# First block, seam and fusion steps of a filter-and-transformer kernel: loads and waits reordered

## Time and profile before

| | us |
|---|---|
| median of 3 runs | 1001.25 (999.52 to 1002.82) |
| the profiled execution | 999.17 |
| its span | 997.3 |
| TensorE busy | 905.2 (91%) |
| VectorE busy | 834.9 (84%) |
| ScalarE busy | 699.3 (70%) |
| GpSimd busy | 122.3 (12%) |
| mean granted clock of TensorE | 0.976 |

### The profile page before, as it was taken

One profiled execution on the slowest core, in us unless ns is written; L12 is line 12 of the kernel. 1 busy time (PEld: TensorE's weight loads), 2 busy tenths in 40 slices (PEclk: granted clock), 3 DMA queues, 4 the chain that ended last, 5 costly groups with the idle time before them and its releaser, 6 DMA issues.

```text
span 997.3 us, 18874 instructions
## 1 busy us (share of the span) xinstructions
PE 905.2 (91%) x6960; PEld 700.2 (70%) x6960; DVE 834.9 (84%) x1160; ACT 699.3 (70%) x2252; POOL 122.3 (12%) x147
## 2 busy tenths in 40 slices
PE   5489999999999999999999997889998999999997
PEld 4267777777777777777777775767675766667675
DVE  2999999999999999999999998987899599352443
ACT  2666876976877877877876875757767686767842
POOL 6201011011011011101101111101010111000000
PEclk9699999999999999999999999999998999999999
DMA  7311120031010121010220010000001000100000
GB/s 173 113 35 28 66 89 19 22 122 45 18 45 17 32 90 39 17 46 14 70 80 11 17 38 11 12 22 12 27 17 38 17 22 17 44 27 2 17 1 32
DMA packets 24925, 39.00 MB, mean 39 GB/s; under 512 B 4001, under 2 KB 20609, under 8 KB 23553
## 3 DMA queue, kind: packets, MB, share of 16 engines
...
q0 software_dynamic: 384, 1.05, 0.5%
...
HBM read 22.21 MB, written 5.24 MB: 28 GB/s over the span
## 4 chain that ended last, share of the span: by engine, by line
DVE 47%; PE 25%; ACT 16%; issue 9%; DMA 2%; POOL 1%; SPq 0%; DVEq 0%; POOLq 0%; ACTq 0%
ACT prob L1086 7%; PE ps_t L849 7%; DVE f L1726 4%; DVE f L1753 4%; PE ps_m L860 4%; DVE f L1748 4%; DVE p L1738 4%; DVE f L1757 4%; DVE neg_max L1762 4%; DVE f L1743 3%; ACT u L1073 3%; DVE f L1721 2%; DVE f L1710 2%; PE ps_s L796 2%; DVE f L1699 2%
## 5 line engine op out<-in xcount | busy, mean ns | idle before, releaser
L1086 ACT ACTIVATE prob<-ps_s,neg_max 128x128 f32<-128x128 f32 x512 | 181.3, 408 | 7.3 <-DVE neg_max L1762 7.3
L1086 ACT ACTIVATION_READ_ACCUMULATOR prob<-ps_s,neg_max 128x1 f32 x512 | 126.6, 249 | 0.0
L655 PE MATMUL ps_t<-w,hidT 128*128 128x256 f32 x512 | 125.7, 383 | 0.0
L1094 ACT ACTIVATE probT<-ps_t 128x512 f32<-128x512 f32 x128 | 81.1, 634 | 44.3 <-PE ps_t L601 28.7
L655 PEld LDWEIGHTS ps_t<-w,hidT 128*128 128x128 f32 x512 | 91.1, 190 | 12.1 <-ACT hidT L1168 3.0
L849 PE MATMUL ps_t<-km,w_fc 128*128 128x384 f32 x256 | 93.9, 503 | 1.0 <-ACT km L1282 1.0
L601 PE MATMUL ps_t<-ident,prob 128*128 128x128 f32 x512 | 81.5, 283 | 12.9 <-ACT prob L1086 6.7
L601 PEld LDWEIGHTS ps_t<-ident,prob 128*128 128x128 f32 x512 | 60.0, 144 | 36.6 <-issue 14.7
L1762 DVE TENSOR_REDUCE neg_max<-ps_s 128x8 f32<-128x1024 f32 x64 | 77.5, 1211 | 4.6 <-PE ps_s L591 4.6
L1341 ACT ACTIVATE prob<-ps_s,neg_max 128x128 f32<-128x128 f32 x192 | 53.8, 376 | 22.6 <-DVE neg_max L1935 22.2
L849 PEld LDWEIGHTS ps_t<-km,w_fc 128*128 128x128 f32 x256 | 47.5, 195 | 26.8 <-issue 3.7
...
## 6 DMA issues: line engine op xcount, KB each, us to landing
...
w_attn<-in_w_attn SPq DMA_DIRECT2D x4, 768.0 KB, 5.4
...
```

The costliest lines, as they stand in the source:

```text
L655: last = mm(ps_t[:, 0, D * t:D * t + D], hidT[:, m, P * t:P * t + P], w2[:, m], start=False, stop=(m == MC - 1), skip_group_check=True)
L1086: last = A(prob[:, n % 2, hh], ps_s[n % 2][:, hh], ACT.Exp, scale=-1.0, bias=neg_max[:, n % 2, hh:hh + 1], accum_out=den)
L1094: A(probT[:, 4 * half:4 * half + 4].rearrange("p h k -> p (h k)"), ps_t[:, 1], ACT.Copy).then_inc(s["act_pT"], 1)
```

## The change

What it does, part by part:

- SP: taps and positions are issued from ScalarE's queue. The filter's column weights (`vf[:, 1]`) come before its row weights, each with a semaphore of its own, and both ahead of the projections, which now stand behind the first row shift. The rest of layer 0's weights moves behind `rows_above(0)`, `w2` behind `rows_above(1)`; the images of the next pair go from a block's first iteration to its second.
- GpSimd: the last six gathers wait for the projections to have landed. The masks are one head wide (`[P, 2, P]`), and their readers repeat them by a broadcast.
- TensorE, SP and ScalarE's first tanh wait for eight constants (`N_EARLY`), not nine; ScalarE's first tanh did not wait for constants before.
- VectorE: `first_step` begins with the head masks and the first filter operations, ahead of the positions; `head_max(0, 0)` to `(0, 2)` move behind other filter operations; in block 0 the two `normalise` stand among the divergence operations; in block 15 they stand ahead of `divergence_out`.
- TensorE: four `hold_clock` ahead of `fuse_queries(0)`, three behind `tile_scores(0, 0)`.
- ScalarE: `values_in(n + 1)` ahead of `norm_y(n)` in `fuse_step`.

```diff
@@ -86,7 +86,7 @@
         ident = sb("ident", [P, P])
         ident_h = sb("ident_h", [P, P], BF16)
         ones = sb("ones", [P, 4 * P])
-        mask = sb("mask", [P, 2, 4, P], BF16)
+        mask = sb("mask", [P, 2, P], BF16)
         head_mask = sb("head_mask", [P, 2])
         pow_half = sb("pow_half", [P, 4])
         row_mask = sb("row_mask", [P, 4])
@@ -251,37 +251,28 @@
-        N_CONST = 8 + 1
+        N_EARLY = 8
+        N_CONST = N_EARLY + 1
...
         @block.sync
         def _(sp):
             sp.dma_start(tokens[:], d["tokens"]).then_inc(s["l_tok"], 16)
-            sp.dma_start(taps[:, 0:18], d["nabla_w"].partition_broadcast(P)).then_inc(s["l_taps"], 16)
-            sp.dma_start(taps[:, 18:36], d["div_w"].partition_broadcast(P)).then_inc(s["l_taps"], 16)
-            sp.dma_start(pe[:], d["pe"]).then_inc(s["l_pe"], 16)
             load_images = lambda k: sp.dma_start(o_all[:, k], d["o"][2 * k:2 * k + 2].rearrange("b (p r) c -> (b p) r c", r=RPP))
             load_images(0).then_inc(s["l_img"], 16)
-            sp.dma_start(w_attn[:, :, 0:3 * D], d["w_attn"][0][:, :, 0:3 * D]).then_inc(s["l_qkv"], 16)
-            for img in range(2):
-                for comp in range(2):
-                    sp.dma_start(vf[64 * img:64 * img + 64, comp], d["vf"][comp].rearrange("(p r) c -> p r c", r=RPP)).then_inc(s["l_vf"], 16)
+            for comp, loaded in ((1, "l_vf"), (0, "l_vf_rows")):
+                for img in range(2):
+                    sp.dma_start(vf[64 * img:64 * img + 64, comp], d["vf"][comp].rearrange("(p r) c -> p r c", r=RPP)).then_inc(s[loaded], 16)
             def rows_below(it):
                 if it < ITERS * PAIRS:
                     sp.wait_ge(s["act_tanh"], it + 1)
                     for at in (0, 64):
                         sp.dma_start(u[at:at + 63, RPP, 0:IMG], u[at + 1:at + 64, 0, 0:IMG]).then_inc(s["halo_u"], 16)
-            sp.wait_ge(s["c_pool"], N_CONST)
+            sp.wait_ge(s["c_pool"], N_EARLY)
             rows_below(0)
-            sp.wait_ge(s["g_emb"], 16 * (B - 2))
-            sp.dma_start(w_attn[:, :, 3 * D:4 * D], d["w_attn"][0][:, :, 3 * D:4 * D]).then_inc(s["l_wc"], 16)
-            sp.dma_start(cols[:], d["cols"]).then_inc(s["l_vec"], 16)
-            sp.dma_start(rows_last[:], d["rows_last"].partition_broadcast(P)).then_inc(s["l_vec"], 16)
-            sp.dma_start(b1[:], d["b1"][0]).then_inc(s["l_bc"], 16)
-            sp.dma_start(w1[:], d["w1"][0]).then_inc(s["l_w1"], 16)
-            sp.dma_start(w2[:], d["w2"][0]).then_inc(s["l_w2"], 16)
+            sp.dma_start(w_attn[:, :, 0:3 * D], d["w_attn"][0][:, :, 0:3 * D]).then_inc(s["l_qkv"], 16)
             sp.wait_ge(s["c_general"], 1)
             which = sp.value_load(general[0:1, 0:1], min_val=0, max_val=1)
...
@@ -348,11 +339,24 @@
+            def first_weights():
+                sp.wait_ge(s["g_emb"], 16 * (B - 2))
+                sp.dma_start(w_attn[:, :, 3 * D:4 * D], d["w_attn"][0][:, :, 3 * D:4 * D]).then_inc(s["l_wc"], 16)
+                sp.dma_start(cols[:], d["cols"]).then_inc(s["l_vec"], 16)
+                sp.dma_start(rows_last[:], d["rows_last"].partition_broadcast(P)).then_inc(s["l_vec"], 16)
+                sp.dma_start(b1[:], d["b1"][0]).then_inc(s["l_bc"], 16)
+                sp.dma_start(w1[:], d["w1"][0]).then_inc(s["l_w1"], 16)
+
+            def first_ff_out():
+                sp.dma_start(w2[:], d["w2"][0]).then_inc(s["l_w2"], 16)
+
             for k in range(BLOCKS):
                 it, its, l = sum(BLOCK_ITERS[:k]), BLOCK_ITERS[k], k // PAIRS
                 for i in range(its):
                     rows_above(it + i)
-                    if i == 0 and k < PAIRS - 1:
+                    if k == 0:
+                        (first_weights if i == 0 else first_ff_out)()
+                    if i == 1 and k < PAIRS - 1:
                         load_images(k + 1).then_inc(s["l_img_rest"], 16)
                     if i == 0 and k % PAIRS == PAIRS - 1 and l + 1 < LAYERS:
                         load_projections(l + 1)
@@ -422,6 +427,7 @@
                 if b == 1:
                     const(pool.memset(v[:], 0.0))
                     assert c == N_CONST
+                    pool.wait_ge(s["l_qkv"], 16)
             pool.wait_ge(s["g_emb_first"], 32)
@@ -432,10 +438,10 @@
             for first in range(2):
                 for half in range(2):
                     m = mask[64 * half:64 * half + 64, first]
-                    const(pool.affine_select(out=m, in_=m, compare_op=ALU.is_gt, fill=MASKED, base=0, pattern=[[0, 4], [1, P]], channel_multiplier=-1))
-                    const(pool.affine_select(out=m, in_=m, compare_op=ALU.is_ge, fill=MASKED, base=WIN, pattern=[[0, 4], [-1, P]], channel_multiplier=1))
+                    const(pool.affine_select(out=m, in_=m, compare_op=ALU.is_gt, fill=MASKED, base=0, pattern=[[1, P]], channel_multiplier=-1))
+                    const(pool.affine_select(out=m, in_=m, compare_op=ALU.is_ge, fill=MASKED, base=WIN, pattern=[[-1, P]], channel_multiplier=1))
                     if first and half == 0:
-                        const(pool.affine_select(out=m, in_=m, compare_op=ALU.is_ge, fill=MASKED, base=-WIN, pattern=[[0, 4], [1, P]], channel_multiplier=0))
+                        const(pool.affine_select(out=m, in_=m, compare_op=ALU.is_ge, fill=MASKED, base=-WIN, pattern=[[1, P]], channel_multiplier=0))
             const(pool.memset(v_f[:, :, :, HD:], 1.0))
             for t in (vT_f[:, 0:WIN], kT_f[:, 0:WIN]):
                 const(pool.memset(t, 0.0))
@@ -709,6 +715,8 @@
                 if a + 1 < BLOCKS:
                     queries(a + 1)
                 else:
+                    for _ in range(4):
+                        hold_clock(BLOCKS)
                     fuse_queries(0)
                     fuse_values(0)
@@ -783,9 +791,9 @@
                 else:
                     pe_.wait_ge(s["f_q"], n + 1)
                     pe_.wait_ge(s["f_k"], n + 1)
-                    m = mask[:, 1].rearrange("p a k -> p (a k)")
+                    m = mask[:, 1].unsqueeze(1).to_broadcast([P, 4, P])
                     for hb in range(2):
-                        mm(quad[hb], ident_h[:], m, start=True, stop=False, skip_group_check=True)
+                        mm(quad[hb].rearrange("p (a k) -> p a k", a=4), ident_h[:], m, start=True, stop=False, skip_group_check=True)
                 for c in range(FKV):
                     for r in range(2):
                         to = P * (2 * c + r)
@@ -869,6 +877,8 @@
                 carry_attn(LAST)
                 project_out(LAST)
                 tile_scores(0, 0)
+                for _ in range(3):
+                    hold_clock(BLOCKS)
                 tile_turn(0, 0, 0)
                 tile_turn(0, 0, 1)
                 turn_ffn(LAST)
@@ -1044,7 +1054,7 @@
                 ff_out(f, 1, range(0, 4))
                 ff_out(f, 2, range(0, 4))
-            pe_.wait_ge(s["c_pool"], N_CONST)
+            pe_.wait_ge(s["c_pool"], N_EARLY)
             for i in range(40):
                 tr(ps_t[:, 1, P * (i % 4):P * (i % 4) + P], ident[:], ident[:])
             first_step()
@@ -1063,6 +1073,10 @@
         def _(act):
             A = act.activation
+            act.dma_start(taps[:, 0:18], d["nabla_w"].partition_broadcast(P)).then_inc(s["l_taps"], 16)
+            act.dma_start(taps[:, 18:36], d["div_w"].partition_broadcast(P)).then_inc(s["l_taps"], 16)
+            act.dma_start(pe[:], d["pe"]).then_inc(s["l_pe"], 16)
+
             def first_tanh(pair):
                 A(u[:, 0:RPP, 0:IMG], o_all[:, pair], ACT.Tanh).then_inc(s["act_tanh"], 1)
@@ -1137,6 +1151,8 @@
                 scaled_rows(k, ps_t[:, 0], rstd, shift).then_inc(s["h_ready"], 1)
             def keys_out(k, g):
+                if k == 0:
+                    act.wait_ge(s["c_heads"], 1)
                 act.wait_ge(s[f"pe_k{g}"], k + 1)
                 for o in range(2):
                     last = A(km[:, g, :, o], quad[2 + g][:, 0:D].rearrange("p (t k) -> p t k", t=2), ACT.Copy, scale=head_mask[:, o:o + 1])
@@ -1252,6 +1268,7 @@
                 filter_out(1)
                 queries_out(1)
+            act.wait_ge(s["c_pool"], N_EARLY)
             act.wait_ge(s["l_img"], 16)
             first_tanh(0)
             act.wait_ge(s["c_general"], 1)
@@ -1344,7 +1361,7 @@
             def tile_mask(n, t):
                 act.wait_ge(s["f_exp"], 2 * TT * n + 2 * t)
                 for hb in range(2):
-                    last = A(quad[hb], mask[:, 0].rearrange("p a k -> p (a k)"), ACT.Copy)
+                    last = A(quad[hb].rearrange("p (a k) -> p a k", a=4), mask[:, 0].unsqueeze(1).to_broadcast([P, 4, P]), ACT.Copy)
                 last.then_inc(s["f_mask"], 1)
             def tile_sink(n, t):
@@ -1456,8 +1473,8 @@
                 x_out(n + 1)
                 z_last(n - 1)
                 keys_biased(n + 1)
+                values_in(n + 1)
                 norm_y(n)
```

(54 more changed lines are left out.)

9 lines of the change are left out of this document (5 added, 4 removed).

## The result

The changed kernel takes **997.07 us** (median; 993.73 to 1002.02), the kernel before beside it 1001.67 (998.75 to 1006.41), in 20 runs each: ratio 0.9949 [0.9935, 0.9962], some 5.1 us faster. Forecast was 992.3, so the sign is right and about four tenths of the gain is missing. The median lies 0.07 above the upper end of the forecast's range (997); the ratio, put on the 1001.25 that the forecast started from, gives 996.1, inside it. The profiled execution took 997.71 with a span of 996.0, 1.3 less than that of the kernel before.

What follows compares the result with a forecast made beforehand. VectorE was taken to lead the chain (47%, TensorE 25%). Gains of 6.9 (head), 0.8 (seam) and 1.2 (fusion steps) sum to 8.9 us, taking the median from 1001.25 to 992.3, range 987.5 to 997.

Steps and rivals of the forecast that it cites:

- The bound: Whole kernel: VectorE leads the chain; what the first block ends earlier, the end of the text stage is earlier.
- the term of 6.9 for the head: Kernel start: earlier loads and new order start block 1's first operation at 52.7 instead of 59.57, 6.9 us earlier.
- the forecast's signs of being wrong: Start, block 0: block 1 starting after 56, keys after 16, or gathers spaced over 2 us.
- so the tanh runs from 5.0 to 6.1: Kernel start: SP issues the image 1.41 us earlier, so ScalarE's first tanh runs from 5.0 to 6.1.
- keys at 13.6: Kernel start: the keys' products begin at 13.6 us, just behind the projections' landing, taken as 13.2.
- Rival 2: Cold TensorE at the start: clock falls before the keys, products up to twice as long; 2.4 lost, 994.7; chance 0.14.
- The 3 us wait ahead of normalise(0, 0): Block 0, at 44 to 47 us: in the new order VectorE waits some 3 us instead of working.
- The seam, 0.8: About 611 to 629 us: fillers and earlier normalise end queries 2.8 earlier; VectorE next in line, so 0.8 kept.
- The swap, 1.2: Fusion steps 2 and 4: value copy ahead of the norm falls into ScalarE's wait, 0.6 each, 1.2 us.
- Rival 1: Kernel start: projections land late, at 18.3, held by row shifts and filter weights; 4.1 lost, 997.2; chance 0.08.
- Rival 3: Block 0: six gathers each wait out a VectorE operation of 1.2, last lands 7 us later; 995.3; chance 0.12.
- Rival 4: Block 0: gathers get nowhere until VectorE pauses at 26; 14.6 lost against 8.9 won, 1006.9; chance 0.03.

Runs made afterwards that it cites:

- experiment 4: Changed kernel with taps and positions issued by SP behind the four filter weights instead of by ScalarE: 1001.41 us, ratio 0.9991 to the kernel before.
- experiment 10: Changed kernel with taps and positions issued by SP ahead of the image, as in the kernel before: 999.79 us, ratio 0.9975 to the kernel before.
- experiment 12: Kernel of experiment 8 with 16 instead of 24 later fillers and the small loads by SP ahead of the image: 991.15 us, ratio 0.9892.
- experiment 8: Changed kernel, table loaded early, block 0's normalises behind divergence_out(1), fillers 64 for 40 plus 24 behind the text rows' turn: 995.18 us, ratio 0.9914.
- experiment 11: Kernel of experiment 8 with small loads ahead of the image and projections issued ahead of the wait for the tanh: 993.18 us, ratio 0.9914.
- experiment 6: Kernel before with only the seam's edit: seven hold_clock fillers, block 15's normalises ahead of divergence_out: 999.82 us, ratio 0.9988.
- experiment 7: Kernel before with only values_in ahead of norm_y in the fusion steps: 1001.88 us, ratio 0.9992.
- experiment 3: Changed kernel with block 0's two normalises put back behind divergence_out(1): 995.88 us, ratio 0.9933 to the kernel before.
- experiment 5: Changed kernel with seam fillers, block 15's normalises and values_in as before, leaving the new start and masks: 1000.58 us, ratio 0.9986.
- experiment 9: Changed kernel without GpSimd's wait for the projections ahead of the last six gathers: 999.89 us, ratio 0.9979 to the kernel before.
- experiment 1: The changed kernel run again, nothing altered: 998.48 us, ratio 0.9962 to the kernel before.
- experiment 2: Changed kernel with a tiny activation ahead of ScalarE's waits, to load the activation table early: 998.55 us, ratio 0.9969 to the kernel before.

## Why the prediction was partly right

**The bound: right.** Block 1's start does carry through. From there to the first tile maximum of the seam the profiles need 562.3 to 564.8 us, whatever the head.

**Failed step: the term of 6.9 for the head.** It was mis-sized by its inputs, not by its chain. Two of the forecast's signs of being wrong came, block 1 after 56 and keys after 16, and of the third, gathers spaced over 2 us, one pair (17.78 and 19.92). Up to the first head maximum, forecast for 19.2 and seen at 25.03, 5.83 us were lost; from there to block 1 I forecast 33.5, and 33.39 was measured. The 5.83 are two items:

- *"so the tanh runs from 5.0 to 6.1" and "keys at 13.6"*: 3.55 us. I moved the image by its issue slot, 1.41, and took its landing with it. No run has that. With the small loads on a second queue beside them, tokens land at 3.93 and the image at 8.21, later than in the kernel before. Without the second queue the image lands at 6.75 when issued at 1.26 (experiment 4), and at 6.38 and 6.58 when issued at 2.67 (the kernel before, experiment 10). So the second queue costs some 1.5 us, and the earlier slot alone gave nothing; what holds the image there was not tried (in experiment 4 a megabyte of filter weights follows it, and the DMA share is 0.93 to 1.11 from 3 to 7 us). The table load of 1.28 then stands behind the image. I had given it "4 us to spare"; the order of the waits took that away, since the first activation now has two and the load starts when one of them ends. The projections landed at 17.15, 4.8 behind their issue: the duration was about right (5.4 taken), the issue 4.6 late. Experiment 10 confirms the loads (tokens 2.44, keys at 15.78), experiment 12 the whole.
- *Rival 2, to which I gave 0.14, came true*: 2.28 us. The first fillers end at 10.1, TensorE sits idle 4.57 us before the turn of the text rows, the clock is at the lower level and the keys and queries take 5.98, not 3.72. In all three profiles with fillers up to the keys (experiments 8, 11 and 12) they take 3.62. My price for it, 2.4, was right; the chance was not, and I left it out of the likeliest case. The kernel before is not safe either: the earlier trace rows has 3.72, but in experiments 6 and 7, whose head is that of the kernel before, the same products take 5.22 and 5.41. There TensorE's pause between the fillers and the turn is 2.83 and 2.58 us, against 1.61 in the kernel before. One profile of a stretch whose clock varies is a poor baseline.

With both mended and the normalises back (experiment 12), block 1 starts at 52.30; the forecast was 52.7, although the parts differ: the maximum at 21.97 is 2.8 late, and the normalises, back in their place, give 3 back.

**The 3 us wait ahead of normalise(0, 0): foreseen.** 3.65 measured, and experiment 3 shows what it costs. The forecast priced it into the sum, correctly.

**The seam, 0.8: right in place, and of the right order in size.** The queries take 2.82 instead of 4.39, in every profile with the fillers. From block 1's start to the first key copy of fusion step 1, the kernel before needs 645.69 and experiment 7 646.53; eight profiles with the seam's edit and without the low clock told of below need 644.5 to 645.4 (mean 644.9), some 1.2 less. That leaves out profiles by what they show: over all eleven with the edit the mean is 645.9, over all three without it (experiment 5 has 647.67, with more low clock in that stretch) 646.6. And the pair that differs in the seam alone, experiment 6 and the kernel before, is 0.3 apart. So the gain lies between 0.3 and 1.2, and the time of experiment 6 cannot tell it from nothing. VectorE is next in line, as said: the first maximum after the seam comes 1.3 us nearer in experiment 6 than in the kernel before, and 1.0 of that is given back in the following step (82.32 against 81.31).

**The swap, 1.2: failed.** "Ahead of the norm that copy falls into the wait: 0.6 each" happened to the digit, and the step after it was missing: I took ScalarE's gain for the chain's, without asking who the tile maximum waits for. It is VectorE, in line. Along VectorE's own order are left of it 0.00 in step 2 and 0.14 in step 4. What the swap may bring is another thing that I had not in view: the products in which TensorE brings the values over no longer wait for `values_in` (in step 4 they follow at once in experiment 7, where the kernel before waits 1.82 us), and in step 4 the clock then mostly stays up. The eleven profiles with the swap average 157.8 us from there to the end against 159.0, so by chance the 1.2 of the forecast; the measured time, 0.08% [−0.11, 0.27], allows that and nothing. That the earlier values keep the clock up was not tested by itself.

**Rival 1** (projections at 18.3) came half true, at 17.15, by late issue and not by a busy queue.

**Rival 3**, gathers held by VectorE, was right in its mechanism and wrong in its size. Of the six later gathers of each of the fourteen profiles, 66 take 0.94 to 0.96 us and 18 take 1.03 to 1.98. All 18 started while VectorE was in a pass over SBUF, 16 with two inputs and two in its multiply of 0.69, and all 18 ended 0.81 to 0.84 us after that pass: the gather at 17.78 above starts in the pass that ends at 18.79 and ends at 19.62. The 66 started with no such pass running or in its last 0.15 us, but for one in experiment 10, which started 0.02 behind the pass. A reduction beside them held none (experiment 12, at 22.27: 0.94). So a gather waits for the rest of the pass in which it starts. It did not do so six times for 1.2 us: gathers follow each other by 1.25 us, about as the passes do, so after one wait most start at the end of a pass. The changed kernel lost 0.9 in all, experiments 4 and 9 some 2. The last was issued at 24.91 and all had landed by 28.7, ahead of the tanh at 35.27, so it cost nothing.

**Rival 4**, no gather until VectorE pauses: false. The Trainium skill, "SBUF — State Buffer", section "Who interferes with whom", says that a VectorE pass with two SBUF inputs holds GpSimd work that reads SBUF; it infers that building a gather's descriptors needs the write side alone, and from that the prediction took it that such a pass holds no gather. The traces bear out the first sentence and speak against what the prediction took from the second, by the 18 gathers.

**What stays open.** How much the head gave. Experiment 5 has 0.14% [−0.07, 0.35], so 1.4 us; the whole, less seam and swap, would leave 3.7; block 1's start in the three profiles with the changed head is 58.42, 61.66 and 61.95, in the three with the old one 59.57, 60.40 and 60.41. The two later ones have 1.5 to 2 us of the idle time described next. By these profiles the head as changed gave nothing on the average. The stretches named above hold some 1.2 us at the seam and 1.2 at the end; the rest of the measured 3.8 to 5.1 is not located. That the total came near the forecast is in part luck: the clock in step 4 was not in it.

## What to carry to other kernels

An earlier issue slot is not an earlier landing: before moving loads to a second queue, ask what then shares the transfer engines with the first ones, and which engine reads each small load first. Follow a gain on one engine to the next instruction that the chain's engine runs; where that engine is in line without a gap, the gain is nothing (the swap). A pause of TensorE ahead of its first products can leave them at the lower clock (pauses of 2.6 to 8.3 us here, products of 5.1 to 6.5 us in place of 3.62): carry fillers right up to the first products, and read the clock of that stretch in several profiles before using its durations. Where a gather is urgent, look at which VectorE pass it starts in: here it waited up to 1.03 us for the end of one.

## What the runs showed beyond the forecast

- **An unexplained gap behind the scores.** In seven of the ten profiles in which text rows were still on their way while the first scores ran, VectorE, idle, began the first head maximum (`head_max(0, 0)`) 1.16 to 2.00 us after the scores' end; in five of them (experiments 1, 2, 3, 8, 10) the row names "remote", that is, the profile found no instruction or DMA that ended the wait. In the other three, and in all four whose rows had landed by then (the kernel before, experiments 6, 7 and 9), it began 0.06 to 0.07 behind. From the changed kernel's second profile:

```profile
24.29 1.15 PE L597 MATMUL ps_s<-km,qT 32*128 32x256 f32 x16 [0.69 <-issue]
...
27.44 1.23 DVE L1784 TENSOR_REDUCE neg_max<-ps_s 128x8 f32<-128x1024 f32 x1 [5.96 <-remote]
```

  Experiment 9 was on record with the gap gone and it was, but one profile against a rate of seven in ten proves little. The traces do say where the time goes: in all fourteen profiles the semaphore that the last product of the scores raises, the one that the maximum waits for, rises 0.02 us before the maximum starts. So it is TensorE's signal that comes late, while TensorE is already at the next products, and not VectorE that hesitates. Why the signal is late, and what rows on their way would do to it, stays open.
- **Low clock that comes and goes at fixed places.** The stretch from the seam's first tile maximum to the next step's key copy takes 82.1 to 82.4 us in eight profiles with the seam's edit and 84.4 to 85.1 in three, among them the changed kernel's first; its granted clock is 0.90 to 0.92 in the three and 0.94 in experiment 6. The end of the kernel has three lengths, as told under experiment 7. Such steps of 2 to 4 us may be why single executions of one kernel lie 8 us apart, and they are why differences of under 2 us needed stretches of the trace and not times.
- **With two waits ahead of the first activation, the table load takes one of them.** With one wait ahead of the first activation it ran at 0.79; with two, behind the image (8.21); with a tiny activation ahead, at 2.18 in experiment 2 and at 0.79 in experiment 12, where ScalarE issues no loads. Moving it early did not give back its 1.28 each time: the tanh came 0.89 earlier in experiment 2 and 1.28 in experiment 8, but only 0.10 in experiment 12 against 10, where the image was there at 7.77 instead of 6.58. Whether that is chance is open.
